# Time-mix and mixture-of-experts kernel: how the last batch's expert rows come back to their tokens

## The chip, the cores and the metric

The kernel runs on one core of one Trainium2 chip. A core has five engines with instruction streams of their own: TensorE (PE, matmuls into the banks of PSUM), VectorE (DVE), ScalarE (ACT), GpSimd (POOL) and SyncE (SP, which here only issues DMAs). They meet through semaphores. Sixteen DMA engines move data between the on-chip memory and DRAM; SP and POOL both hand them work. The metric is the device time of one launch in microseconds, median of three runs.

## The reference, cut to what matters

```python
x = layernorm(x + time_mix(x))            # (4, 1024, 128), two layers, a scan over time in each
# per batch of 1024 tokens: 8 experts, the best K = 2 for each token, cap = int(1.2*2*1024/8) = 307 slots
top2, ei = top_k(x @ router_w + router_b, 2);  probs = softmax(top2)
pos = running count of each expert's picks, all first choices before all second ones
expert_inputs = zeros(8, cap, 128).at[ei, pos].add(x)
o = (silu((xe @ w_fc + b_fc) * (xe @ w_gate + b_gate)) @ w_proj) + b_proj
y[token] = sum over k of probs[k] * o[ei[k], pos[k]]      # an index past cap reads row cap - 1
out = layernorm(x + y)
```

## The kernel before

Four batches go through the kernel one behind another. After a head (time mixing of batches 0 and 1, weights split into a high and a low part), the program is four **passes**, one for each batch. A pass has 32 **points**: point 4e + j computes columns 128j to 128j + 127 of the hidden layer of expert e, as six matmuls into a pair of PSUM banks (`hidden_pair`), a copy with bias on ACT (`gate_copy`), and a product on DVE (`product`, L1053), which frees the banks for the point after next. Four tables (`TENSOR_...`, `SCALAR_...`, `VECTOR_...` and POOL's own) say what else each engine does at which point: time mixing of the batch after next, routing of the next batch, and the combining of batches already computed. So the order is written out by hand on each engine, and a wait on one instruction holds all that stand behind it.

The way of a batch b through DRAM has four legs:

- **Scatter** (POOL, `scatter`, L1160): 16 indirect DMAs write the tokens' normalized rows `x_ln` into `slot_rows` by expert slot, one for 128 tokens and one of their two choices. They stand at points 9 to 24 of pass b - 1. SP then loads `slot_rows` in five groups (`load_slots`, L386), PE turns three of these at points 28 to 30, and two in the next pass.
- **Store** (SP, `store_expert`, L394): each expert's 312 slots by 128 outputs are copied from PSUM by DVE (`copy_out`, L1062, as 104 partitions by 3 rows, in a ring of three buffers `o_sb`) and stored plainly into `expert_rows`. The copy of expert e stands at point 4(e + 2); those of experts 6 and 7 stand at points 0 and 2 of the next pass, or behind the last pass.
- **Gather** (POOL, `gather`, L1182): 16 indirect DMAs bring back, for 128 tokens and one choice each, the rows that these tokens need, from `expert_rows` into `picked`. The first waits until all eight experts are stored. A gather into quarter q of `picked` also waits until the earlier output of that quarter has been stored.
- **Combine** (`gather_sum`, L1018 to L1034, and `final_norm`, L1041, on DVE; `final_rstd`, L1193 and L1197, on POOL; `store_out`, L398, on SP): share times row plus `x_ln`, mean and variance, normalization, output, by quarters of two tiles of 128 tokens.

Batches 0 to 2 gather and combine inside later passes. For batch 3 nothing is left to hide behind: its 16 gathers stand after pass 3 on POOL, then its combining, then four output stores.

POOL is kept in step with the points by `pace(b, point)`, which waits for the product of the point before. `FILL` lists spare matmuls that PE runs at a few places where it would stand idle.

## Time and profile before

| | us |
|---|---|
| median of three runs | 389.23 (389.17 to 389.45) |
| the profiled execution: its own time | 389.6 |
| the profiled execution: span from first to last instruction | 387.9 |
| busy in the span: PE, DVE, POOL, ACT | 323.1, 261.8, 186.8, 168.3 |
| chain that ended last: PE 55%, DVE 14%, issue 11%, POOL 8%, DMA 6%, ACT 4% of the span | |
| the 64 gathers (L1182) on POOL: busy, mean of one | 66.2, 1.035 |
| the 64 scatters (L1160) on POOL: busy, mean of one | 72.0, 1.125 |

The span leaves out what lies around the first and the last instruction, 1.7 us here. PE is busy for 83% of the span, but that is an average: in the last tenth it hardly works. The share by engine of the chain says how the span was spent when each moment is put down to what the end depended on. Busy time of POOL for an indirect DMA is only the time in which POOL prepares it; the data move afterwards.

### The profile page before, as it was taken

The numbers are of one execution on the slowest core, as the hardware profiler recorded it, in microseconds if no ns is written. First come the engines' busy times: TensorE is split into PE (matmuls) and PEld (weight loads), VectorE is DVE, ScalarE is ACT, GpSimd is POOL, SyncE is SP. The second block draws the span as 40 slices with busy tenths as digits, with TensorE's granted clock in tenths as the row PEclk, the third lists the DMA queues.
The fourth block names the chain that finished last, engine by engine and source line by source line (L and its number), as shares of the span: only waits on it lengthen the run. The fifth ranks groups of instructions, "written<-read, shape, count | busy, mean of one in ns | idle before, by whom it ended". The sixth has DMA issues, their size and how long they took to land.

```text
span 387.9 us, 6844 instructions
## 1 busy us (share of the span) xinstructions
PE 323.1 (83%) x2193; PEld 269.7 (70%) x2193; DVE 261.8 (68%) x846; ACT 168.3 (43%) x309; POOL 186.8 (48%) x225
## 2 busy tenths in 40 slices
PE   6978877679899999999999999989999897795000
PEld 3434544346888969999798899989989797794000
DVE  6496774767966877979788778894546775751234
ACT  2535424444554544545446453545454544451000
POOL 5021315772234473324646557747746667200674
PEclk9999969999999999999999999999999999999555
DMA  7615963414013113211111161123262132121112
GB/s 221 186 55 58 199 184 93 130 36 140 3 32 97 37 47 112 71 41 46 49 44 48 44 184 54 49 64 100 76 178 78 41 96 76 48 60 33 41 50 71
DMA packets 53058, 31.73 MB, mean 82 GB/s; under 512 B 12704, under 2 KB 48807, under 8 KB 53024
## 3 DMA queue, kind: packets, MB, share of 16 engines
q1 hardware_dynamic: 47840, 22.99, 21.8%
q0 software_dynamic: 4096, 8.06, 7.2%
q10 hardware_dynamic: 1088, 0.26, 0.4%
q8 instruction: 17, 0.28, 0.3%
q14 instruction: 17, 0.14, 0.1%
HBM read 18.92 MB, written 12.71 MB: 82 GB/s over the span
## 4 chain that ended last, share of the span: by engine, by line
PE 55%; DVE 14%; issue 11%; POOL 8%; DMA 6%; ACT 4%; SPq 0%; DVEq 0%; POOLq 0%; ACTq 0%
PE ps_o L647 14%; POOL slot_rows L1160 4%; POOL picked L1182 3%; PE bank L499 3%; PE bank L507 3%; DMA picked<-expert_rows,row_from 2%; PE bank L509 2%; PE pair0g L633 2%; DVE prod L1053 2%; DVE kv_sb L899 2%; DMA slot_rows<-x_ln,row_to 2%; PE pair1h L578 2%; PE bank L611 2%; PE pair1g L633 2%; DMA slot_x<-slot_rows 2%
## 5 line engine op out<-in xcount | busy, mean ns | idle before, releaser
L647 PE MATMUL ps_o<-proj_sb,hidden 128*104 128x128 f32 x744 | 94.0, 274 | 2.1 <-DVE o_sb L1062 2.1
L1160 POOL DMA_INDIRECT slot_rows<-x_ln,row_to x64 | 72.0, 1125 | 42.9 <-DVE prod L1053 24.4
L1182 POOL DMA_INDIRECT picked<-expert_rows,row_from x64 | 66.2, 1035 | 53.4 <-DVE prod L1053 18.7
L647 PEld LDWEIGHTS ps_o<-proj_sb,hidden 128*104 128x104 f32 x744 | 87.3, 170 | 4.1 <-issue 2.5
L772 ACT ACTIVATE gate_s<-pair0g,bgate_sb 128x308 f32<-128x308 f32 x64 | 33.1, 516 | 81.5 <-PE pair0g L635 81.5
L1053 DVE SCALAR_TENSOR_TENSOR prod<-pair1h,bfc_sb,gate_s 128x308 f32<-128x308 f32 x64 | 34.0, 531 | 23.3 <-ACT gate_s L772 22.8
L779 ACT ACTIVATE hidden<-prod 128x616 f32<-128x616 f32 x64 | 45.5, 710 | 9.3 <-DVE prod L1053 9.3
L1053 DVE SCALAR_TENSOR_TENSOR prod<-pair0h,bfc_sb,gate_s 128x308 f32<-128x308 f32 x64 | 34.0, 531 | 19.7 <-ACT gate_s L772 18.9
L772 ACT ACTIVATE gate_s<-pair1g,bgate_sb 128x308 f32<-128x308 f32 x64 | 32.9, 514 | 20.1 <-PE pair1g L635 19.6
L1135 POOL TENSOR_SCALAR shifted<-moments 128x4 f32<-128x4 f32 x24 | 5.6, 231 | 69.2 <-DVE moments L856 69.1
L633 PE MATMUL pair1g<-slotT_hi,gate_hi 128*128 128x308 f32 x64 | 26.1, 408 | 4.9 <-DVE prod L1053 4.9
L633 PE MATMUL pair0g<-slotT_hi,gate_hi 128*128 128x308 f32 x64 | 25.6, 400 | 0.9 <-DVE prod L1053 0.5
L1139 POOL TENSOR_TENSOR rstd<-shifted,power 128x4 f32<-128x4 f32 x24 | 25.0, 1041 | 2.0
L1018 DVE SCALAR_TENSOR_TENSOR picked<-picked,share,x_ln 128x128 f32<-128x128 f32 x30 | 9.2, 346 | 20.3 <-DMA picked<-expert_rows,row_from 20.3
L1062 DVE TENSOR_TENSOR o_sb<-ps_o,bproj_sb 104x384 f32<-104x384 f32 x32 | 17.5, 547 | 6.6 <-PE ps_o L647 3.2
L930 DVE TENSOR_TENSOR slotT_lo<-bank,slotT_hi 128x512 fp32r<-128x512 f32 x20 | 13.8, 689 | 11.9 <-ACT slotT_hi L756 11.7
L578 PE MATMUL pair1h<-x_ln,ident 128*128 128x512 f32 x32 | 17.0, 613 | 5.8 <-ACT fc_hi L763 4.2
L899 DVE TENSOR_TENSOR_SCAN kv_sb<-decay,kv_sb 128x512 f32<-128x512 f32 x16 | 20.0, 1253 | 0.4
L635 PE MATMUL pair1g<-slotT_hi,gate_lo 128*128 128x308 f32 x64 | 19.5, 305 | 0.0
L633 PE MATMUL pair0h<-slotT_hi,fc_hi 128*128 128x308 f32 x64 | 19.5, 305 | 0.0
L634 PE MATMUL pair1h<-slotT_lo,fc_hi 128*128 128x308 f32 x64 | 19.5, 305 | 0.0
L633 PE MATMUL pair1h<-slotT_hi,fc_hi 128*128 128x308 f32 x64 | 19.5, 305 | 0.0
(155 smaller groups left out, 725.5 us busy)
## 6 DMA issues: line engine op xcount, KB each, us to landing
slot_x<-slot_rows SPq DMA_DIRECT2D x20, 256.0 KB, 3.3
expert_rows<-o_sb SPq DMA_DIRECT2D x32, 156.0 KB
x_in<-in_L_attn_h SPq DMA_DIRECT2D x4, 512.0 KB, 4.8
x_ln<-in_L_ffn_w_gate SPq DMA_DIRECT2D x8, 256.0 KB, 3.7
x_ln<-in_L_ffn_w_c_fc SPq DMA_DIRECT2D x8, 256.0 KB, 4.1
proj_sb<-in_L_ffn_w_c_proj SPq DMA_DIRECT2D x8, 256.0 KB, 5.4
out<-picked SPq DMA_DIRECT2D x16, 128.0 KB, 2.1
slot_rows<-slot_x SPq DMA_DIRECT2D x5, 256.0 KB, 4.4
```

The costliest lines, as they stand in the source:

```text
L578: nc.tensor.matmul(pair[1][1][:, :], ident[:, :], w_in[:, e % 2, H * which:H * which + H], start=True, stop=False)
L633: nc.tensor.matmul(ps, hi[:, e, chunk], slotT_hi[:, cols], start=True, stop=False)
L634: nc.tensor.matmul(ps, hi[:, e, chunk], slotT_lo[:, cols], start=False, stop=False)
L635: nc.tensor.matmul(ps, lo[:, e, chunk], slotT_hi[:, cols], start=False, stop=True).then_inc(made, 1)
L647: mm = nc.tensor.matmul(ps_o[0:PART, P * part:P * part + P], hidden[:, e % 2, c, PART * part:PART * part + PART], proj_sb[:, e, c, :], sta ...
L772: nc.scalar.activation(gate_s[:, c % 2, :], pair[c % 2][0][:, 0:COLS], ACT.Identity, bias=bgate_sb[:, e, j:j + 1]).then_inc(g_copied, 1)
L779: nc.scalar.activation(hidden[:, e % 2, 2 * i:2 * i + 2, 0:COLS], prod[:, e % 2, 2 * i:2 * i + 2, :], ACT.Silu).then_inc(hidden_made, 1)
L899: nc.vector.tensor_tensor_scan(kv_sb[:, lo:hi], decay[:, :], kv_sb[:, lo:hi], kv_sb[:, lo - 1:lo] if n % 2 else 0.0, ALU.mult, ALU.add)\
L1053: nc.vector.scalar_tensor_tensor(prod[:, e % 2, j, :], pair[c % 2][1][:, 0:COLS], bfc_sb[:, e, j:j + 1], gate_s[:, c % 2, :], ALU.add, ALU ...
L1139: nc.gpsimd.tensor_tensor(rstd[:, r, norm, tiles], shifted[:, r, norm, tiles], power[:, 0:HT], ALU.pow)\
L1160: nc.gpsimd.indirect_dma_start(out=slot_rows, out_offset=bass.IndirectOffsetOnAxis(ap=row_to[:, c:c + 1], axis=0), in_=x_ln[:, b % RING, c ...
L1182: nc.gpsimd.indirect_dma_start(out=picked[:, j, k, :], out_offset=None, in_=expert_rows[b % 2], in_offset=bass.IndirectOffsetOnAxis(ap=row ...
```

## The change

The last batch (`LAST`, pass 3) takes another way back. Its expert outputs are not stored by slot and gathered by token, but **sent** by slot to the place of their token, and then loaded plainly.

1. Each row of `x_ln`, of the slot buffer and of `slot_rows` becomes 129 numbers long. The additional one (`homes`) is the token's place in a new DRAM tensor `returned` (2048 rows of 128, two for each token), or a far value for batches 0 to 2 and for empty slots. So the scatter carries each slot's home along. The expert weights that are loaded into the same memory in the head now land in pieces of 128 numbers.
2. SP loads these numbers (`load_homes`, 104 by 24 numbers of 4 bytes each from rows 516 bytes apart) at the end of pass 2. DVE adds 1 where the slot's number is not below the count of first choices of its expert (`homes_of`); PE gets this count by 8 more matmuls in `count`.
3. DVE clears a buffer at point 14 of pass 2 (`blank`) and SP writes it twice over `returned` (1 MB in all, `blank_returned`), after the store of expert 4 and ahead of the slot loads of batch 3.
4. In pass 3 POOL sends each expert's three times 104 rows (`send_back`) at points 4(e + 2) to 4(e + 2) + 2, those of experts 6 and 7 behind the pass. SP stores no `expert_rows` there, but moves one row of each expert, the one that tokens past the capacity read (`load_last_row`).
5. Tokens past the capacity get their share of that row by a matmul: `over_of` on DVE, `turn_over` and `add_over` on PE, `copy_over` on ACT.
6. Behind the pass SP loads `returned` in four plain DMAs of 256 KB (`load_picks`). PE adds up in PSUM: `keep` puts in `x_ln` (identity times tile), `add_picks` adds two products for each tile with diagonal matrices of the shares (`scales_of`, 128 by 1024 each, on DVE at points 12 and 16). DVE takes statistics and norm from PSUM (`last_stats`, `last_norm`). Twenty spare matmuls stand before `add_picks`.
7. The combining of batch 2 moves: its gathers stand at points 4 to 7 and 9, 11, ... 31 of pass 3, its sums of quarters 0 to 2 at points 10, 18 and 26 (they were at 10, 14, 18 and 22), and the fourth behind the pass. The gathers of batch 1 move from pass 3 into pass 2 (points 21 to 31). In pass 2 the scatters are allowed at points 9 to 20 in place of 9 to 24.
8. `picks`, `y_out`, `scale` and others lie in memory that is free by then (`x_mid`, `x_in`, `mixed`, `kv_sb`), and `x_ln` has a buffer for each batch, as before (four).

```diff
-RING = 4
+RING = B
...
-GATHERS_LAST = {**{p: (2, 12 + p) for p in range(0, 4)}, **{p: (1, p - 4) for p in range(4, 20)}}
+GATHERS_LAST = {**{p: (1, p - 4) for p in range(4, 8)}, **{9 + 2 * i: (1, 4 + i) for i in range(12)}}
+GATHERS_AHEAD = {**{p: (2, 12 + p) for p in range(0, 4)}, **{p: (1, p - 4) for p in range(4, 9)},
+                 **{p: (1, p - 16) for p in range(21, 32)}}
 POOL_COMBINE = {10: [(1, 0)], 29: [(1, 1)], 3: [(2, 2)], 7: [(2, 3)]}
-POOL_COMBINE_LAST = {3: [(2, 2)], 7: [(2, 3)], 10: [(1, 0)], 14: [(1, 1)], 18: [(1, 2)], 22: [(1, 3)]}
+POOL_COMBINE_LAST = {1: [(2, 2)], 5: [(2, 3)], 11: [(1, 0)], 19: [(1, 1)], 27: [(1, 2)]}
...
+RETURNS = {4 * (e + 2) + i: (e, i) for e in range(6) for i in range(PARTS)}
+TENSOR_LAST = {9: [("keep", 0)], 11: [("keep", 1)], 20: [("turn_over", 0)], 22: [("turn_over", 1)], 24: [("keep", 2)]}
+SCALAR_LAST = {21: [("copy_over", 0)], 23: [("copy_over", 1)]}
+VECTOR_LAST = {1: [("over", 0)], 5: [("homes", 0)], 12: [("scales", 0)], 16: [("scales", 1)]}
...
-        x_ln = sb("x_ln", [P, RING, TILES, P])
+        x_rows = sb("x_rows", [P, RING, TILES, P + 1])
+        x_ln = x_rows[:, :, :, 0:P]
+        homes = x_rows[:, :, :, P:P + 1]
...
-        slot_x = sb("slot_x", [P, SLOT_RING, 4, P])
+        slot_in = sb("slot_in", [P, SLOT_RING, 4, P + 1])
+        slot_x = slot_in[:, :, :, 0:P]
...
+        picks = x_mid[:, :, :, :].rearrange("p r (o j) d -> p (r o) j d", j=K)
+        y_out = x_in[:, 1, :, :]
+        overs = row_in[:, 0:TILES * E]
+        oversT = normT[0:E, :]
+        last_rows = normed[0:E, 0, :]
+        scale = [held[:, :].rearrange("p (j d) -> p j d", d=P) for held in (mixed, kv_sb)]
...
-                sp.dma_start(w_in[:, e % 2, 0:H], w_gate[e]).then_inc(expert_weights_in[e % 2], 16)
-                sp.dma_start(w_in[:, e % 2, H:2 * H], w_fc[e]).then_inc(expert_weights_in[e % 2], 16)
+                sp.dma_start(w_in[:, e % 2, 0:HC, :], w_gate[e].rearrange("p (j d) -> p j d", d=P)).then_inc(expert_weights_in[e % 2], 16)
...
+            def load_homes():
+                sp.wait_ge(scattered, nth(LAST, 16 * TILES * K, 16 * TILES * K))
+                with nc.allow_non_contiguous_dma("one number of each row"):
+                    sp.dma_start(home_f[:, :], home_view).then_inc(home_in, 16)
+            def blank_returned():
+                sp.wait_ge(blank_made, 1)
+                for i in range(2):
+                    sp.dma_start(blank_view[i], x_in[:, 0, :, :].rearrange("p j d -> p (j d)"))\
+                      .then_inc(returned_blank, 16)
+            def load_last_row(e):
+                sp.wait_ge(o_copied, nth(LAST, E, e + 1))
+                i = (LAST * E + e) % OUT_RING
+                sp.dma_start(last_rows[e:e + 1, :], o_sb[LAST_ROW:LAST_ROW + 1, i, LAST_PART, :])\
+                  .then_inc(last_row_in[i], 16)
+            def load_picks(q):
+                for i in range(OUT_RING):
+                    sp.wait_ge(sent_back[i], 16 * PARTS * last_experts(i))
+                sp.dma_start(picks[:, QT * q:QT * q + QT, :, :].rearrange("p j k d -> p j (k d)"),
+                             returned_view[:, QT * q:QT * q + QT, :]).then_inc(picks_in[q], 16)
...
+                    for j in range(TILES):
+                        mm = nc.tensor.matmul(route_banks(b)[1][:, TILES * K * E:TILES * K * E + E], ones[:, :],
+                                              chosen[:, j, 0, :], start=False, stop=(j == TILES - 1),
+                                              skip_group_check=True)
...
+            def keep(q):
+                if q < 3:
+                    pe.wait_ge(slots_copied, nth(LAST, GROUPS, (3, 4, 5)[q]))
+                if q == 2:
+                    pe.wait_ge(over_copied, 2)
+                if q == 3:
+                    pe.wait_ge(g_copied, nth(LAST, POINTS, POINTS - 1))
+                for i in range(QT):
+                    nc.tensor.matmul(sums(q)[:, P * i:P * i + P], ident[:, :], x_ln[:, LAST, QT * q + i, :],
+                                     start=(i == 0), stop=False, skip_group_check=True)
+            def turn_over(half):
+                pe.wait_ge(over_step, 3)
+                if half == 0:
+                    pe.wait_ge(slots_copied, nth(LAST, GROUPS, 5))
+                else:
+                    pe.wait_ge(over_copied, 1)
+                for i in range(HT):
+                    j = HT * half + i
+                    mm = nc.tensor.transpose(bank[1][0:E, P * i:P * i + P], overs[:, E * j:E * j + E], ident[:, :])
+                mm.then_inc(over_turned, 1)
+            def add_over(q):
+                if q == 0:
+                    for i in range(OUT_RING):
+                        pe.wait_ge(last_row_in[i], 16 * last_experts(i))
+                for i in range(QT):
+                    j = QT * q + i
+                    nc.tensor.matmul(sums(q)[:, P * i:P * i + P], oversT[:, P * j:P * j + P], last_rows,
+                                     start=False, stop=False, skip_group_check=True)
+            def add_picks(q):
+                pe.wait_ge(scale_made, 2)
+                pe.wait_ge(picks_in[q], 16)
+                for i in range(QT):
+                    j = QT * q + i
+                    for k in range(K):
+                        mm = nc.tensor.matmul(sums(q)[:, P * i:P * i + P], scale[k][:, j, :], picks[:, j, k, :],
+                                              start=False, stop=(k == K - 1), skip_group_check=True)
+                mm.then_inc(summed, 1)
...
+            keep(QUARTERS - 1)
+            for q in range(QUARTERS):
+                add_over(q)
+            pe.wait_ge(g_copied, nth(LAST, POINTS, POINTS))
+            fill("picks", LAST, 0, pair[1][0])
+            for q in range(QUARTERS):
+                add_picks(q)
...
+            def blank():
+                dve.wait_ge(normed_made[1], step(LAST - 1, 5))
+                nc.vector.memset(x_in[:, 0, :, :], 0.0).then_inc(blank_made, 1)
...
+                nc.vector.tensor_tensor(second[:, :].rearrange("p (e i) -> p e i", i=PARTS),
+                                        place[:, :].rearrange("p (e i) -> p e i", i=PARTS),
+                                        firsts[0:PART, :].rearrange("p (e o) -> p e o", o=1).to_broadcast([PART, E, PARTS]),
+                                        ALU.is_ge).then_inc(home_step, 1)
+                dve.wait_ge(home_step, 1)
+                dve.wait_ge(home_in, 16)
+                nc.vector.tensor_tensor(second[:, :], second[:, :], home_f[:, :], ALU.add).then_inc(home_step, 1)
+                dve.wait_ge(home_step, 2)
+                nc.vector.tensor_copy(home[:, :], second[:, :]).then_inc(home_made, 1)
...
+            def scales_of(k):
+                nc.vector.tensor_tensor(scale[k], ident[:, :].rearrange("p (o d) -> p o d", o=1).to_broadcast([P, TILES, P]),
+                                        share[:, LAST, :, k:k + 1].to_broadcast([P, TILES, P]), ALU.mult)\
+                  .then_inc(scale_made, 1)
...
+            def last_stats(q):
+                dve.wait_ge(summed, q + 1)
+                for i in range(QT):
+                    mm = nc.vector.bn_stats(y_stats[:, QT * q + i, :], sums(q)[:, P * i:P * i + P])
+                mm.then_inc(y_stats_made, 1)
+                dve.wait_ge(y_stats_made, nth(LAST, QUARTERS, q + 1))
+                for j in range(QT * q, QT * q + QT):
+                    mm = nc.vector.bn_aggr(y_moments[:, j, :], y_stats[:, j, :])
+                mm.then_inc(y_moments_made, 1)
...
-                    in_=x_ln[:, b % RING, c // K, :], in_offset=None, bounds_check=ROWS - 1, oob_is_err=False)\
+                    in_=x_rows[:, b, c // K, :], in_offset=None, bounds_check=ROWS - 1, oob_is_err=False)\
                   .then_inc(scattered, 16)
+            def send_back(e, i):
+                c = LAST * E + e
+                if e == 0 and i == 0:
+                    pool.wait_ge(home_made, 1)
+                    pool.wait_ge(returned_blank, 16 * 2)
+                if i == 0:
+                    pool.wait_ge(o_copied, nth(LAST, E, e + 1))
+                nc.gpsimd.indirect_dma_start(
+                    out=returned,
+                    out_offset=bass.IndirectOffsetOnAxis(ap=home[:, PARTS * e + i:PARTS * e + i + 1], axis=0),
+                    in_=o_sb[:, c % OUT_RING, i, :], in_offset=None, bounds_check=K * T - 1, oob_is_err=False)\
+                  .then_inc(sent_back[c % OUT_RING], 16)
...
+            nc.gpsimd.memset(slot_in[:, 0, :, P:P + 1], FAR).then_inc(zeroed, 1)
...
+            nc.gpsimd.memset(homes[:, 0:LAST, :, :], FAR).then_inc(homes_made, 1)
+            nc.gpsimd.iota(homes[:, LAST, :, :].rearrange("p j o -> p (j o)"), pattern=[[K * P, TILES]], base=0,
+                           channel_multiplier=K, allow_small_or_imprecise_dtypes=True).then_inc(homes_made, 1)
+            nc.gpsimd.iota(place[:, :], pattern=[[0, E], [PART, PARTS]], base=0, channel_multiplier=1,
+                           allow_small_or_imprecise_dtypes=True).then_inc(homes_made, 1)
...
-            for c in range(K * TILES):
-                gather(B - 1, c)
+            for e in range(E - 2, E):
+                for i in range(PARTS):
+                    send_back(e, i)
+            final_rstd(LAST - 1, QUARTERS - 1)
```

The order of POOL in pass 3, before, points 4 to 14. The names: `picked<-expert_rows` is a gather, `returned<-o_sb` a send, `y_shifted` and `y_rstd` are the two instructions of one `final_rstd`.

```order
L1182 DMA picked<-expert_rows,row_from 128x128 x4
L1193 TENSOR_SCALAR y_shifted<-y_moments 128x2
L1197 TENSOR_TENSOR y_rstd<-y_shifted,power 128x2
L1182 DMA picked<-expert_rows,row_from 128x128 x3
L1193 TENSOR_SCALAR y_shifted<-y_moments 128x2
L1197 TENSOR_TENSOR y_rstd<-y_shifted,power 128x2
L1182 DMA picked<-expert_rows,row_from 128x128 x4
```

And after, the same engine, points 4 to 13 of pass 3.

```order
L1423 DMA picked<-expert_rows,row_from 128x128 x2
L1433 TENSOR_SCALAR y_shifted<-y_moments 128x2
L1437 TENSOR_TENSOR y_rstd<-y_shifted,power 128x2
L1423 DMA picked<-expert_rows,row_from 128x128 x2
L1400 DMA returned<-o_sb,home 2048x128
L1423 DMA picked<-expert_rows,row_from 128x128
L1400 DMA returned<-o_sb,home 2048x128 x2
L1423 DMA picked<-expert_rows,row_from 128x128
L1433 TENSOR_SCALAR y_shifted<-y_moments 128x2
L1437 TENSOR_TENSOR y_rstd<-y_shifted,power 128x2
L1400 DMA returned<-o_sb,home 2048x128
L1423 DMA picked<-expert_rows,row_from 128x128
```

Where one gather stood at each point up to point 19, there are now, from point 8 to the end of the pass, two gathers and three sends for every four points.

The end of POOL's program, before.

```order
L1182 DMA picked<-expert_rows,row_from 128x128 x16
L1193 TENSOR_SCALAR y_shifted<-y_moments 128x6
L1197 TENSOR_TENSOR y_rstd<-y_shifted,power 128x6
L1193 TENSOR_SCALAR y_shifted<-y_moments 128x2
L1197 TENSOR_TENSOR y_rstd<-y_shifted,power 128x2
```

And after; the row of six sends is experts 6 and 7.

```order
L1400 DMA returned<-o_sb,home 2048x128 x2
L1423 DMA picked<-expert_rows,row_from 128x128
L1400 DMA returned<-o_sb,home 2048x128 x6
L1433 TENSOR_SCALAR y_shifted<-y_moments 128x2
L1437 TENSOR_TENSOR y_rstd<-y_shifted,power 128x2
L1433 TENSOR_SCALAR y_shifted<-y_moments 128x6
L1437 TENSOR_TENSOR y_rstd<-y_shifted,power 128x6
L1433 TENSOR_SCALAR y_shifted<-y_moments 128x2
L1437 TENSOR_TENSOR y_rstd<-y_shifted,power 128x2
```

Sixteen gathers behind the pass became six sends, and one `final_rstd` of batch 2 came in behind them.

SP around the boundary of passes 2 and 3, before: `expert_rows<-o_sb` is an expert's store, `slot_x<-slot_rows` a slot load.

```order
L394 DMA expert_rows<-o_sb 104x3x128 x2
L386 DMA slot_x<-slot_rows 128x4x128 x3
L394 DMA expert_rows<-o_sb 104x3x128
L386 DMA slot_x<-slot_rows 128x4x128 x2
L394 DMA expert_rows<-o_sb 104x3x128 x3
```

And after.

```order
L480 DMA expert_rows<-o_sb 104x3x128 x2
L459 DMA returned<-x_in 128x1024 x2
L449 DMA slot_in<-slot_rows 128x4x129 x3
L480 DMA expert_rows<-o_sb 104x3x128
L449 DMA slot_in<-slot_rows 128x4x129 x2
L454 DMA home_f<-slot_rows 104x24x1
L480 DMA expert_rows<-o_sb 104x3x128 x2
```

The two writes of 512 KB came in ahead of the slot loads, and the load of the homes behind them.

## Rows read from the trace of the kernel before

**Rows 1.** Two windows at the end: busy us and instructions by engine, clock, DMA, GB/s.
```profile
300.00:340.00 40.00, 33.93 (x258) 32.37 (x258) 27.99 (x87) 18.39 (x35) 23.57 (x30) 1.00 0.25 67
...
352.00:388.00 36.00, 2.62 (x24) 2.41 (x23) 10.88 (x41) 0.00 (x0) 18.84 (x20) 0.58 0.19 53
```

**Rows 2.** Timeline, last 37 us: start, us, engine, line, operation [idle before, releaser].
```profile
351.14 0.56 DVE L1062 TENSOR_TENSOR o_sb<-ps_o,bproj_sb 104x384 f32<-104x384 f32 x1
...
351.75 2.87 PE L661 MATMUL ps_o<-proj_sb,hidden 128*104 128x128 f32 x24 [0.65 <-DVE o_sb L1062]
354.65 0.56 DVE L1062 TENSOR_TENSOR o_sb<-ps_o,bproj_sb 104x384 f32<-104x384 f32 x1 [2.96 <-PE ps_o L661]
358.10 1.11 POOL L1182 DMA_INDIRECT picked<-expert_rows,row_from  x1 [18.02 <-DMA expert_rows<-o_sb]
...
367.19 0.49 DVE L1030 BATCH_NORM_STATS2 y_stats<-picked 128x6 f32<-128x128 f32 x2
...
367.71 0.25 DVE L1034 BATCH_NORM_AGGREGATE y_moments<-y_stats 128x2 f32<-128x6 f32 x2
...
379.04 1.00 POOL L1182 DMA_INDIRECT picked<-expert_rows,row_from  x1 [0.30 <-issue]
...
380.48 1.36 POOL L1197 TENSOR_TENSOR y_rstd<-y_shifted,power 128x6 f32<-128x6 f32 x1
381.55 0.35 DVE L1072 SCALAR_TENSOR_TENSOR picked<-picked,share,x_ln 128x128 f32<-128x128 f32 x1 [1.22 <-DMA picked<-expert_rows,row_from]
...
382.75 2.13 DVE L1041 TENSOR_SCALAR picked<-picked,y_moments,y_rstd 128x128 f32<-128x128 f32 x8
...
383.25 0.79 POOL L1197 TENSOR_TENSOR y_rstd<-y_shifted,power 128x2 f32<-128x2 f32 x1
383.36 1.98 SPq L398 DMA_DIRECT2D out<-picked  x4
```

**Rows 3.** Chain that ended last, two stretches: start us, us, what.
```profile
85.27 2.77 DMA slot_rows<-x_ln,row_to
...
279.68 3.81 DMA slot_rows<-x_ln,row_to
...
283.51 2.83 DMA slot_x<-slot_rows
```

**Rows 4.** Timeline of POOL, passes 2 and 3.
```profile
259.31 1.03 POOL L1160 DMA_INDIRECT slot_rows<-x_ln,row_to  x1 [0.31 <-issue]
...
279.68 0.97 POOL L1160 DMA_INDIRECT slot_rows<-x_ln,row_to  x1 [0.30 <-issue]
...
313.68 1.11 POOL L1182 DMA_INDIRECT picked<-expert_rows,row_from  x1 [2.70 <-DVE prod L1053]
...
317.45 0.23 POOL L1193 TENSOR_SCALAR y_shifted<-y_moments 128x2 f32<-128x2 f32 x1
317.77 0.72 POOL L1197 TENSOR_TENSOR y_rstd<-y_shifted,power 128x2 f32<-128x2 f32 x1
318.69 1.17 POOL L1182 DMA_INDIRECT picked<-expert_rows,row_from  x1 [0.20 <-issue]
```

**Rows 5.** Timeline of DVE, pass 3: a sum waits for its gather.
```profile
321.53 0.61 DVE L1018 SCALAR_TENSOR_TENSOR picked<-picked,share,x_ln 128x128 f32<-128x128 f32 x2 [1.95 <-DMA picked<-expert_rows,row_from]
```

**Rows 6.** Timeline of SP, the second store of batch 1.
```profile
310.73 0.93 SPq L398 DMA_DIRECT2D out<-picked  x2
```

**Rows 7.** Page, DMA queues and issues: packets, MB, share; KB, us to landing.
```profile
q1 hardware_dynamic: 47840, 22.99, 21.8%
...
bfc_sb<-in_L_ffn_b_c_fc SPq DMA_DIRECT2D x1, 16.0 KB, 5.0
```

**Rows 8.** Lines of DVE: names, shapes, count, busy us, mean ns, idle.
```profile
L880 DVE TENSOR_TENSOR x_in<-x_in,x_mid 128x1024 f32<-128x1024 f32 x4 | 4.9, 1217 | 0.0
```

**Rows 9.** Windows of 2 us: granted clock is the third number from the right.
```profile
356.00:358.00 2.00, 0.00 (x0) 0.00 (x0) 0.00 (x0) 0.00 (x0) 0.00 (x0) 1.00 0.29 80
358.00:360.00 2.00, 0.00 (x0) 0.00 (x0) 0.00 (x0) 0.00 (x0) 1.11 (x1) 0.50 0.05 16
```

More of the change, by code:

```diff
@@ L669, in period @@
                     hidden_pair(b, e, j)
+                    if b == LAST:
+                        for name, n in TENSOR_LAST.get(point, ()):
+                            last_stages[name](n)
                     if b + 1 < B:
@@ L1096, in period @@
                             slots_low(b + ahead, g)
+                    if b + 1 == LAST and point == 14:
+                        blank()
+                    if b == LAST:
+                        for name, n in VECTOR_LAST.get(point, ()):
+                            last_stages[name](n)
                     for name, behind, q in (VECTOR_COMBINE if b + 1 < B else VECTOR_COMBINE_LAST).get(point, ()):
```

172 lines of the change are left out of this document (125 added, 47 removed).

## The prediction

> **What bounds the kernel now.** I read the windows first. From 300 to 340 us PE is busy for 33.9 of 40 us; from 352 us on for 2.6 of 36, while POOL is busy for 18.8 and DVE for 10.9 [rows 1]. So the last tenth of the span has another limit than the rest, and the change aims at it. The timeline says which: DVE copies the last expert's outputs at 354.65, POOL starts its first gather at 358.10 and its sixteenth at 379.04, and all of DVE's work there waits for gathers [rows 2]. A gather costs POOL 1.00 us and 0.30 before the next. Behind the sixteenth come its landing (DVE starts at 381.55), sum and statistics, `final_rstd`, the norms (to 384.88) and the output store, 3.0 us to the span's end at 387.9 [rows 2]. From the end of the last copy (355.21) to the end of the span it is 32.7 us, about 21 of it POOL's issuing of gathers.
>
> The chain shows what else the end hangs on. POOL issues scatters without a gap worth naming from 259.31 to 279.68; the last one has landed after 3.81 us, the first slot load takes 2.83, and only then PE can turn slots for pass 3 [rows 3, 4]. Whatever delays scatter or load there delays everything behind.
>
> **The change part by part: the tail.** Removed are the last store with its wait (355.21 to 358.10) and 16 gathers. In their place is a queue of sends on POOL, most of it beside PE's work in pass 3. When does that queue end?
>
> Before, the first gather of batch 2's second quarter starts at 313.68 though it stands at point 8; POOL had waited 2.7 us [rows 4]. I put the wait down to the output stores issued at 310.73 [rows 6], for which this gather must wait and which the changed kernel has at the same place. From there POOL has 12 gathers, 3 `final_rstd` and 17 sends in the pass, and 6 sends behind it. A gather is 1.31 us with its gap. A `final_rstd` took 317.45 to 318.69, with the gap, 1.24 [rows 4], say 1.27. A send of 104 rows is not in the trace. Its upper bound is a scatter of 128 rows, 0.97 + 0.31 = 1.28 [rows 4]; its lower bound is 104/128 of the 0.97, and the gap, 1.10. I take 1.20, the middle, a little up since the first DMA behind another kind of work takes 0.1 more (1.11 and 1.17 against 1.00) [rows 2, 4]. Sum: 12 x 1.31 + 3 x 1.27 + 17 x 1.20 + 6 x 1.20 = 15.7 + 3.8 + 20.4 + 7.2 = 47.1 us. With the start at 313.7 the queue ends at 360.8; the bounds of the send make it 358.5 to 362.6. The other condition is the last copy: it ends at 355.2, and three sends behind it end at 358.8. So POOL's queue decides, by 2 us. Whatever PE or DVE lose in pass 3 up to 2 us is then hidden.
>
> The Trainium skill (DMA: Bandwidth & Descriptors, section "Anatomy of one DMA") puts the cost of generating descriptors down as small, with a fixed part that does not grow with size. By that a send costs what a scatter of 128 rows costs, and the sum ends 23 x 0.08 = 1.8 us later than with my value. No row here has another number of rows than 128.
>
> Behind the queue:
> - The last send starts 1.2 before the end of the queue and has landed 2.8 later (2.77 for a scatter in the head; 3.81 beside gathers is the upper bound) [rows 3]: 362.4.
> - Four loads of 256 KB. The nearest row is a slot load of the same size, 2.83 to its landing [rows 3]. The data of one are 512 packets, at 28.3 ns each on one of 16 engines (21.8% of 16 x 387.9 us over 47,840 packets [rows 7]) 0.9 us; `returned` has pieces twice as long, so 0.8. The fourth is there at 362.4 + 2.8 + 3 x 0.8 = 367.6, the third at 366.8.
> - Each quarter needs four matmuls of 128 x 128 (2.87/24 = 0.12 each, with fill-in and fill-out 0.6) and 0.49 + 0.25 + gaps of statistics, 0.8 [rows 2]. Third quarter's moments 368.2, fourth's 369.0.
> - `final_rstd` of three quarters: 0.23 + 1.36 and gaps, 1.9 [rows 2, 4], to 370.1; of the fourth 0.23 + 0.79 and gaps, 1.1, to 371.2. Then two norms, 0.7: 371.9.
> - 3.0 to the span's end as before: 374.9.
>
> The other work of the tail lies beside the sends and loads: the combining of batch 2's fourth quarter (2 us of DVE at 356, one `final_rstd` behind the sends, before 362.4), `keep`, `add_over` and the 20 spare matmuls on PE. The last row's move lands at about 358 (a store issued behind the last copy, at 355.2, lets POOL go at 358.10 [rows 2]), then 8 matmuls and 20 spare ones, 5 to 6 us at full clock, 364, before the first picks (365.2).
>
> TensorE's granted clock was 1.00 up to 358 and 0.50 behind it, with PE idle since 354.62 [rows 2, 9]. PE now works again at about 358, so the fall may come or not; if `add_picks` runs at 1.2 GHz in place of 2.4, it costs 0.5.
>
> **The rest of the program.**
> - Head: POOL has one more small clearing before the constants that PE's first matmul waits for, 0.2. The weights land in pieces of 512 bytes in place of 2048; the loads are waited for once, so 0 to 0.5. I take 0.3 for both.
> - Boundary of passes 2 and 3: 8 small matmuls and a copy in the routing, on the way to the scatters, 0.3. The scatters are allowed earlier, but POOL already runs them back to back [rows 4], so nothing comes of that. The 1 MB of blank rows is issued at about 279.2, in the very microsecond of the last scatters. At 28.3 ns for 512 bytes it would take 3.6 us of all engines, so it is through at about 284; the last scatters share the engines with it, and the first slot load is issued at 283.5. Bounds 0 and 3.6; I take 0.8, because most of the time is covered by the scatter's own 3.81. The rows of 516 bytes make load and scatter longer by 1% by size; 0 to 0.5, I take 0.2.
> - The homes are 2496 numbers of 4 bytes; 4096 such numbers of the biases took 5.0 us to land [rows 7]. Issued at about 290 they are there at 296, and DVE wants them at point 5, after 303. Nothing, covered by 7 us.
> - Pass 3, DVE: the two `scales_of` are as long as the 1.22 us of a 128 x 1024 addition [rows 8], the small ones 1.5 together; one combining of 2 us leaves the pass, and before it two waits for gathers (1.95 is one) [rows 5]. PE gets about 22 small matmuls, 2 us. But the sum at point 18 now needs the fourth gather from 313.7, behind 3 gathers, 5 sends and a `final_rstd`: start 313.7 + 3.9 + 6.0 + 1.3 = 324.9, landed at 327.5, where DVE would ask for it at about 324. So DVE waits 3 us there. This is the new wait; the pass as a whole ends about where it ended, since DVE's sums of before took as much. I take +0.5 for the last copy, hidden behind POOL's queue.
>
> What moves POOL's start at 313.7 moves the end: 0.3 + 0.3 + 0.8 + 0.2 = 1.6, less 0.4 for the sums at points 1 and 5, which now stand where DVE idles anyway: **+1.2**. Span 374.9 + 1.2 = 376.1; with the 1.7 us around it 377.8, to be held against 389.6 of the profiled execution, which is 0.4 above the median of the runs (389.23). So **377.4 us**, 11.8 less than before.
>
> The Trainium skill (same page, section "How a descriptor splits into AXI transactions") speaks against rows of 516 bytes: a transaction starts at a 256-byte boundary, so a row that starts elsewhere costs additional ones (its example of 576 bytes goes from 18 beats to 25). By that the 0.9 us of data of a slot load would become up to 1.4, and the boundary 0.5 later than by size, the end with it. No row here has rows that start off such a boundary.
>
> **The rivals.**
> 1. POOL's queue in pass 3 is too full. A send costs 1.28 or more (gather and send in turn, each 0.1 dearer), DVE's waits at points 18 and 26 grow, and the last copy slips by more than 2 us. For it: POOL has 5 DMAs, 6.2 us, in four points; from the sum of point 14 (321.53) to the copy behind point 31 (351.14) [rows 2, 5] a point takes 1.7, four of them 6.9, and every second four have a `final_rstd` of 1.3 too. Against: the queue may lag to the end of the pass at no cost. Sends at 1.28 alone give 379.2, the rest up to 381.5.
> 2. The transfers at the boundary. Blank rows ahead of slot loads, 4-byte pieces ahead of the store of expert 6, each on the same queue: the full 3.6 and another 1 or 2. Against: there the engines are mostly idle. 381 to 383.
> 3. The tail is cheaper: sends at 1.10 and the start not moved. Then the last copy decides: 374 to 375.
> 4. Slower. Rows of 129 numbers are cut in two, so that a scatter costs POOL twice the preparation. Place: POOL's run of 16 scatters to 279.68, which is on the chain, and the last five in the head. Price 0.97 x 21 = 20 us: 397. It decides from 0.6 us more for each scatter (12/21). For it: no row has such a length. Against: the work is by row, and their number stays.
> 5. The change does not take the gathers off the end: with the order above that cannot be; six sends stand there.
>
> **How the numbers follow.** Forecast 0.58 (376 to 379), rival 1 0.20, rival 2 0.10, rival 3 0.07, rival 4 with all that loses over 12 us 0.04, something that eats the gain just so 0.01. The range of eight in ten leaves out rival 4 and the ends of 2 and 3: 374.2 to 382. Under 0.2% (0.8 us) a measurement can't tell a change from none. Faster 0.95, same 0.01, slower 0.04.
>
> **What would show it.** The last POOL DMA starts at 360 to 363, not at 379; the sends' mean is 0.8 to 1.0 us; the first `picks` matmul starts at about 366; behind the last norm 3 us. DVE waits at point 18 for `picked`. PE's first slot turn of pass 3 starts at 287 to 288. The forecast is wrong if a scatter's mean leaves 0.97, if the slot turn comes after 289.5, or if PE's busy share of pass 3 falls under that of rows 1.

## The result, and the profile after

The changed kernel took **385.55 us** (median of four runs, 382.97 to 385.58) beside 389.34 for the kernel before (389.17 to 391.3): ratio 0.9862, 95% interval 0.9833 to 0.9891, so 1.4% faster. I had forecast 377.4 with a range of 374.2 to 382.0: the direction was right, the size was not. Two thirds of the 11.8 us did not come. The profiled execution took 385.53, its span is 383.7.

The page first: busy time, then POOL's three kinds of indirect DMA (line, engine, operation, count, busy us, mean ns, idle before).

```profile
PE 340.7 (89%) x2293; PEld 283.0 (74%) x2293; DVE 261.5 (68%) x840; ACT 169.3 (44%) x311; POOL 196.1 (51%) x237
...
L1388 POOL DMA_INDIRECT slot_rows<-x_rows,row_to x64 | 71.5, 1117 | 43.5 <-DVE prod L1224 22.8
...
L1423 POOL DMA_INDIRECT picked<-expert_rows,row_from x48 | 50.3, 1047 | 29.3 <-DVE prod L1224 16.8
...
L1400 POOL DMA_INDIRECT returned<-o_sb,home x24 | 25.4, 1058 | 7.1 <-issue 6.2
```

A scatter costs POOL what it cost (1.125 before), and a send of 104 rows as much as a gather of 128, 1.058. The last POOL DMA now starts at 365.72 and not at 379.04 [rows 2]; I had said 360 to 363. The chain shows two places that are late, and the first is far from the tail. Chain that ended last, start and duration:

```profile
280.69 6.16 DMA slot_rows<-x_rows,row_to
286.86 3.16 DMA slot_in<-slot_rows
...
365.72 2.12 DMA returned<-o_sb,home
...
368.88 4.50 DMA x_mid<-returned
```

The last scatter of batch 3 took 3.81 us to land before [rows 3], and takes 6.16 now. What SP issued meanwhile, and what PE met, in the timeline:

```profile
280.69 0.90 SPq L459 DMA_DIRECT2D returned<-x_in  x2
286.86 1.48 SPq L449 DMA_DIRECT2D slot_in<-slot_rows  x3
...
290.15 1.07 PE L711 MATMUL bank<-ident,slot_in 128*128 128x128 f32 x4 [3.38 <-DMA slot_in<-slot_rows]
```

The 1 MB of blank rows (L459) is issued in the same instant as the last scatter, and the DMA engines are full behind it (the last two numbers are their mean busy share and GB/s):

```profile
282.00:284.00 2.00, 2.00 (x20) 2.00 (x18) 0.78 (x2) 1.07 (x2) 1.70 (x2) 1.00 1.06 412
```

In the kernel before, the same window has a share of 0.13 and 35 GB/s. At 412 GB/s 1 MB takes 2.5 us, an estimate from this row, and the landing is 2.35 longer. PE waits 3.38 us for slots (0.87 before) and turns them at 290.15, beyond the 289.5 that I had named as the mark of a wrong forecast. Right behind the wait its clock is down (windows of 2 us; the clock is the third number from the right), and later once more, in the middle of `add_picks`:

```profile
290.00:292.00 2.00, 1.84 (x8) 1.88 (x9) 0.10 (x1) 0.60 (x1) 1.70 (x2) 0.54 0.89 251
292.00:294.00 2.00, 2.00 (x12) 2.00 (x12) 1.13 (x2) 0.52 (x1) 1.18 (x2) 0.60 0.81 225
...
372.00:374.00 2.00, 1.69 (x9) 1.42 (x8) 1.34 (x8) 0.00 (x0) 0.00 (x0) 0.52 0.71 233
```

The first `product` of pass 3 comes 5.3 us later than before; at the end of pass 2 the two kernels were 1.2 apart. So the boundary, from the end of pass 2 to the first product of pass 3, costs 4.1 us. Pass 3 makes some of it up: from 300 to 340 us PE is busy for 38.76 of 40 us where it was 33.93 [rows 1], and the last `copy_out` starts at 357.62, 3.0 later than before. But POOL can't make it up. It waits for the product of its point and is behind from there (timeline of POOL; the gather at 316.14 answers to the one at 313.68 in [rows 4]):

```profile
307.54 1.11 POOL L1423 DMA_INDIRECT picked<-expert_rows,row_from  x1 [2.45 <-DVE prod L1224]
...
316.14 1.03 POOL L1423 DMA_INDIRECT picked<-expert_rows,row_from  x1 [0.61 <-issue]
...
365.72 0.99 POOL L1400 DMA_INDIRECT returned<-o_sb,home  x1 [0.31 <-issue]
```

Then the tail, in place of [rows 2]:

```profile
367.89 1.91 SPq L471 DMA_DIRECT2D x_mid<-returned  x4
...
370.71 0.46 PE L807 MATMUL bank<-x_mid,mixed 128*128 128x128 f32 x2 [2.68 <-DMA x_mid<-returned]
...
373.52 0.77 PE L807 MATMUL bank<-x_mid,mixed 128*128 128x128 f32 x2 [0.31 <-DMA x_mid<-returned]
...
376.86 1.35 POOL L1437 TENSOR_TENSOR y_rstd<-y_shifted,power 128x6 f32<-128x6 f32 x1
...
378.25 2.00 DVE L1300 TENSOR_SCALAR x_in<-bank,y_moments,y_rstd 128x128 f32<-128x128 f32 x6 [0.94 <-POOL y_rstd L1437]
...
380.17 0.72 DVE L1300 TENSOR_SCALAR x_in<-pair0g,y_moments,y_rstd 128x128 f32<-128x128 f32 x2
```

From the issue of the loads to the end of the span it is 15.8 us; I had 12.5. So the gap between forecast and trace has two halves: the loads are issued 4.3 late (367.89 against 363.6), and what follows them takes 3.3 more.

### The profile page after: what moved, and what is told of

It reads as the page before. It is cut to its first block, busy times and chain, and to the rows that moved or that the text cites. A ratio compares the mean times of both kernels' runs of the same rounds, so it can differ in the third digit from the quotient of the medians.

```text
span 383.7 us, 7087 instructions
## 1 busy us (share of the span) xinstructions
PE 340.7 (89%) x2293; PEld 283.0 (74%) x2293; DVE 261.5 (68%) x840; ACT 169.3 (44%) x311; POOL 196.1 (51%) x237
## 4 chain that ended last, share of the span: by engine, by line
PE 60%; DVE 12%; issue 9%; DMA 8%; POOL 7%; ACT 4%; SPq 0%; DVEq 0%; POOLq 0%; ACTq 0%
PE ps_o L747 16%; PE bank L594 3%; PE bank L602 3%; DMA slot_rows<-x_rows,row_to 2%; PE pair0g L733 2%; PE bank L604 2%; POOL slot_rows L1388 2%; POOL returned L1400 2%; PE pair1g L733 2%; DVE kv_sb L1067 2%; DVE prod L1224 2%; PE pair0g L735 2%; DMA slot_in<-slot_rows 2%; PE pair0g L734 2%; PE bank L711 2%
## 5 line engine op out<-in xcount | busy, mean ns | idle before, releaser
L1388 POOL DMA_INDIRECT slot_rows<-x_rows,row_to x64 | 71.5, 1117 | 43.5 <-DVE prod L1224 22.8
L1423 POOL DMA_INDIRECT picked<-expert_rows,row_from x48 | 50.3, 1047 | 29.3 <-DVE prod L1224 16.8
L1400 POOL DMA_INDIRECT returned<-o_sb,home x24 | 25.4, 1058 | 7.1 <-issue 6.2
L1098 DVE TENSOR_TENSOR slotT_lo<-bank,slotT_hi 128x512 fp32r<-128x512 f32 x20 | 13.8, 689 | 15.1 <-ACT slotT_hi L913 14.9
L678 PE MATMUL pair1h<-x_rows,ident 128*128 128x512 f32 x32 | 17.0, 613 | 5.8 <-ACT fc_hi L920 4.2
L735 PE MATMUL pair1h<-slotT_hi,fc_lo 128*128 128x308 f32 x64 | 19.6, 306 | 0.0
```

Source lines behind the costliest of these rows:

```text
L735: nc.tensor.matmul(ps, lo[:, e, chunk], slotT_hi[:, cols], start=False, stop=True).then_inc(made, 1)
L1388: nc.gpsimd.indirect_dma_start(out=slot_rows, out_offset=bass.IndirectOffsetOnAxis(ap=row_to[:, c:c + 1], axis=0), in_=x_rows[:, b, c // K ...
L1400: nc.gpsimd.indirect_dma_start(out=returned, out_offset=bass.IndirectOffsetOnAxis(ap=home[:, PARTS * e + i:PARTS * e + i + 1], axis=0), in ...
L1423: nc.gpsimd.indirect_dma_start(out=picked[:, j, k, :], out_offset=None, in_=expert_rows[b % 2], in_offset=bass.IndirectOffsetOnAxis(ap=row ...
```

## The experiments

Theory A: the blank rows hold up the last scatters, the boundary slips by 4, and POOL's queue hands that on to the end; its queue is 3 to 4 us longer than I reckoned. The rivals were rows of 516 bytes as the cost (B), another limit behind POOL's queue (C), a delay that needs these rows or the fuller queue beside the writes (D), and, later, on a send's price: it does not depend on its rows (E), or it falls with them (F).

**early_blank**: the same writes half a pass earlier.

```diff
-                    if e == 4 and b + 2 == B:
+                    if e == 1 and b + 2 == B:
                         blank_returned()
...
-                    if b + 1 == LAST and point == 14:
+                    if b + 1 == LAST and point == 2:
                         blank()
```

> The changed kernel, with the clearing at point 2 and the two 512 KB writes over the place rows at expert 1 (point 12) of pass 2 in place of expert 4 (point 24). Theory A: these writes, issued in the microsecond of the last scatters, share the 16 DMA engines with them and stand in front of the slot loads, and so made the boundary 4 us longer. Then the last scatter lands 3.8 us after its start again (6.2 with the change), PE waits about 1 us for the first slots in place of 3.4, the granted clock does not fall there, and the last send on POOL starts 2 to 4 us earlier: 381.5 to 383.5 us. Theory B: the boundary is longer through the rows of 516 bytes or the 4-byte loads of the homes. Then landing and wait stay as they are: 385 to 386 us.

Measured: 380.09 us (380.01 to 380.2), ratio 0.9739 [0.9716, 0.9761] to the kernel before. Its chain at the boundary:

```profile
280.87 3.67 DMA slot_rows<-x_rows,row_to
284.56 2.62 DMA slot_in<-slot_rows
...
287.32 0.63 PE bank L711 x4
```

The landing is back at 3.7, PE waits 0.59, and its clock stays up there. The window from 282 to 284 has a DMA share of 0.35 and 91 GB/s. The first product of pass 3 is 0.85 behind the kernel before in place of 5.3, the last send starts at 361.35 in place of 365.72 (4.4 earlier), the loads are issued at 363.53, and the end is 14.9 behind that in place of 15.8, since `add_picks` ran at full clock. So A holds, and moving two lines of SP and DVE work gave 5.3 us of span, more than I had expected (380.09 lies under my 381.5 to 383.5): I had left out what the lowered clock costs. The boundary shows what the queue does with a delay: here pass 3 starts 4.4 earlier and POOL ends 4.4 earlier.

**before_with_blank**: the kernel before with these writes and nothing else of the change.

```diff
+            def blank_returned():
+                sp.wait_ge(blank_made, 1)
+                for i in range(2):
+                    sp.dma_start(blank_view[i], x_in[:, 0, :, :].rearrange("p j d -> p (j d)"))\
+                      .then_inc(returned_blank, 16)
...
+                    if e == 4 and b + 2 == B:
+                        blank_returned()
```

> The kernel before, with nothing of the change but the 1 MB of blank rows (cleared at point 14 of pass 2, written behind the store of expert 4; nobody reads them). Theory A (these writes alone hold up the last scatters): the last scatter lands about 6.2 us after its start in place of 3.8, the first slot turn of pass 3 starts 2 to 3.5 us later than in the kernel before (286.5), TensorE's clock falls at the boundary as in the changed kernel, and the end is 3.5 to 5 us later: 393 to 395. Theory D (the delay needs the 516-byte rows or POOL's fuller queue as well): landing and turn stay within 1 us, 389 to 390.5.

Measured: 395.71 us (395.03 to 396.97) against 390.34, ratio 1.013 [1.009, 1.017]. Chain and timeline at the boundary:

```profile
283.18 6.22 DMA slot_rows<-x_ln,row_to
289.42 3.11 DMA slot_x<-slot_rows
...
292.66 1.04 PE bank L623 x4
```

In the profiled execution TensorE's clock fell at 101.6 us as well, before any blank row, which put everything behind it 3.5 late (0.54 in the window 101 to 108); that part is not the edit's. From the end of pass 2 to the first product of pass 3 it lost another 4.3 us, with PE waiting 3.56 and its clock at 0.68 and 0.50 in the windows behind. So the writes do it alone; wide rows and a fuller queue aren't needed. Of the 4.3, 2.4 is the landing (6.22 against 3.81), 0.3 the load (3.11 against 2.83), and the rest falls in the stretch at the low clock. D fell. The ratio gives 5.1 us in all, a little over the 3.5 to 5 expected; how much of it the writes cost in the three executions that were not profiled (395.03 to 396.19) is open. The full DMA engines of the window above fit writes and scatter sharing the engines; no run tells this from contention in the DRAM.

**wide_rows**: the kernel before with rows of 129 numbers, and weights in pieces of 128.

```diff
-        x_ln = sb("x_ln", [P, RING, TILES, P])
+        x_rows = sb("x_rows", [P, RING, TILES, P + 1])
+        x_ln = x_rows[:, :, :, 0:P]
...
-        slot_rows = nc.dram_tensor("slot_rows", [ROWS, P], F32, kind="Internal").ap()
+        slot_rows = nc.dram_tensor("slot_rows", [ROWS, P + 1], F32, kind="Internal").ap()
```

> The kernel before, with the rows of 129 numbers alone (x_ln, slot buffer, slot_rows, the weights landing in 512-byte pieces), nothing of the new way back. Theory A: it costs the 0.8 us seen at the start of pass 0 and 0.1 to 0.3 at each boundary: 390.1 to 391 us. Theory B (the rows make scatters and slot loads slow): about 4 us more at the last boundary: 393 to 394 us.

Measured: 391.81 us (390.38 to 394.51) against 389.95, ratio 1.0041 [1.0022, 1.006]: 1.6 us by the ratio, 1.9 by the medians, between the two expectations. The boundary shows none of it: last scatter to landing 3.69, load 2.91 (3.81 and 2.83 before), slot turn at 285.95. B fell. What the profiled execution lost came behind point 16 of pass 3, in a stretch at the low clock. Just ahead of it PE had waited for DVE, which had waited 1.86 for a gather (the wait of [rows 5]):

```profile
323.75 0.41 PE L636 MATMUL pair1g<-slotT_hi,gate_hi 128*128 128x308 f32 x1 [2.25 <-DVE prod L1056]
```

```profile
322.00:324.00 2.00, 0.25 (x2) 0.26 (x3) 1.93 (x8) 0.27 (x1) 1.59 (x4) 1.00 0.18 33
...
324.00:326.00 2.00, 2.00 (x15) 2.00 (x14) 1.50 (x5) 0.97 (x2) 1.72 (x2) 0.78 0.54 135
326.00:328.00 2.00, 2.00 (x10) 2.00 (x10) 0.36 (x2) 0.99 (x2) 1.48 (x2) 0.50 0.42 86
```

The kernel before waits 2.00 us at the same matmul, and there the clock stayed at 1.00. So rows of 516 bytes cost about nothing where I looked for them. They may cost that a wait of 2.0 becomes one of 2.25 and the clock falls behind it, but no run shows that the rows are the reason. Whether that is the whole 1.6 stays open too: one execution was profiled, and the kernel before itself ranged from 389.2 to 392.5 in these comparisons.

**late_gathers**: the last four gathers of batch 2 go behind the last send, and this quarter is combined between the statistics and the norms of batch 3. That takes four instructions, 5.4 us, out of POOL's queue ahead of the last send. (With own semaphores and small buffers, left out here.)

```diff
-GATHERS_LAST = {..., **{9 + 2 * i: (1, 4 + i) for i in range(12)}}
+GATHERS_LAST = {..., **{9 + 2 * i: (1, 4 + i) for i in range(8)}}
...
-            final_rstd(LAST - 1, QUARTERS - 1)
+            for c in range(K * QT * (QUARTERS - 1), K * TILES):
+                gather(LAST - 1, c)
```

> The changed kernel, with the last four gathers of batch 2 (points 25, 27, 29, 31) behind the last send, and the combining of that quarter between the statistics and the norms of batch 3. Theory A: POOL's queue sets the end, so the last send starts up to 5.4 us earlier (4 x 1.34), but not before the last copy and two sends, so near 361.5 in place of 365.7; the quarter's sum on DVE gives 1 us back: 381 to 383 us. Theory C: what counts is fixed behind the last copy (loads, statistics, norms), and the queue is not on the path: 385 us or more, since DVE has 3 us more to do at the end.

Measured: 381.43 us (380.46 to 382.22), ratio 0.9771 [0.9746, 0.9796]. The last send starts at 361.90, 3.8 earlier, with the boundary as slow as in the changed kernel (landing 6.07). So POOL's queue had set the time of the last send: C fell. Of the 5.4 us taken out 3.8 came at the last send, because the queue is now short enough to meet another limit. POOL waits for the copy of expert 6, and behind it stand six sends without a gap (timeline of POOL):

```profile
355.41 0.99 POOL L1446 DMA_INDIRECT returned<-o_sb,home  x1 [1.88 <-DVE o_sb L1247]
...
361.90 0.99 POOL L1446 DMA_INDIRECT returned<-o_sb,home  x1 [0.30 <-issue]
```

The late gathers and the second combining cost 0.5 of it back (16.3 from loads to end in place of 15.8).

**early_and_late**: both edits together, those of early_blank and of late_gathers.

> Both of the above. If boundary and queue are two costs (theory A), pass 3 is earlier by up to 4 us and POOL's queue no longer decides: the last copy does, and two sends behind it: 378 to 380.5 us. If the two are one cost (the queue only hides what the boundary gives), it is as late_gathers alone: 381 to 383 us.

Measured: **377.86 us** (377.3 to 378.27), ratio 0.9685 [0.9663, 0.9708]: 3.15% faster than the kernel before, just under the 378 to 380.5 of theory A, and the best of this study. The two gains add up for the most part: the span is 383.7 with neither edit, 378.4 and 380.4 with one, 375.5 with both (8.2 of 5.3 + 3.3; by the medians 7.7 of 5.5 + 4.1). Two different causes, then, in one queue:

```profile
357.15 0.99 POOL L1446 DMA_INDIRECT returned<-o_sb,home  x1 [0.31 <-issue]
...
359.34 1.91 SPq L479 DMA_DIRECT2D x_mid<-returned  x4
...
370.55 2.29 SPq L496 DMA_DIRECT2D out<-x_in  x4
```

POOL's wait for the copy of expert 6 is there too (1.89 at 350.64), and from this send to the last one it is five steps of 1.30. So the limit has moved: from POOL's queue through the whole pass to PE's and DVE's time for expert 6 and the six sends behind it. By this row a fifth instruction moved out of the queue would bring nothing; it wasn't run.

**short_sends**: sends of 64 rows in place of 104. Rows 64 to 103 of each third are not sent back, so this part of the result is left out.

```diff
-                    out_offset=bass.IndirectOffsetOnAxis(ap=home[:, PARTS * e + i:PARTS * e + i + 1], axis=0),
-                    in_=o_sb[:, c % OUT_RING, i, :], in_offset=None, ...
+                    out_offset=bass.IndirectOffsetOnAxis(ap=home[0:64, PARTS * e + i:PARTS * e + i + 1], axis=0),
+                    in_=o_sb[0:64, c % OUT_RING, i, :], in_offset=None, ...
```

> The changed kernel with sends of 64 rows in place of 104: rows 64 to 103 of each third are not sent back (that part of the result is left out). Theory E (what POOL spends on an indirect DMA does not depend on the rows): the sends' mean stays at 1.00 to 1.06, the last send starts at 365 to 366, the time stays within 0.5 of 385.5. Theory F (it grows with the rows, as my lower bound of 104/128 supposed): the mean falls to about 0.65, 23 sends are 9 us shorter, and the last copy decides when the last send starts (about 361): 380 to 381.5.

Measured: 379.86 us, a single execution. Its sends on the profile's page, and the last ones in the timeline:

```profile
L1400 POOL DMA_INDIRECT returned<-o_sb,home x24 | 22.5, 936 | 7.0 <-issue 6.1 <-DVE o_sb L1236 0.6 <-DVE prod L1224 0.3
...
358.88 0.90 POOL L1400 DMA_INDIRECT returned<-o_sb,home  x1 [0.31 <-issue]
...
361.30 0.90 POOL L1400 DMA_INDIRECT returned<-o_sb,home  x1 [0.30 <-issue]
```

A send behind a send takes 0.90 in place of 0.99: 40 rows fewer save 0.09 to 0.10 us, 2.4 ns a row, and if the two sizes are taken as a line, an estimate, some 0.75 us are left that don't depend on rows. (The line does not reach the scatters and gathers, which take 0.97 and 1.00 for 128 rows.) The mean of 0.936 is under E's 1.00 to 1.06, but far from F's 0.65: a small part grows with the rows. Yet the time fell as F had it. The trace gives the parts: the span is 5.6 shorter, of which 1.6 is an earlier start of the gather that I reckon from (314.55 in place of 316.14; the landing at the boundary took 5.45 this time, though nothing there was edited), 2.8 POOL's queue from there to the last send (46.75 in place of 49.58), 0.1 the landing, and 1.1 behind the loads, with `add_picks` at full clock. So my expectation for E was wrong in its time: 24 sends at 0.12 less are 2.9 us, and I had put 0.5. Some 0.9 of these 2.9 are one send, the sixth, which takes 1.83 to 1.85 in each profiled execution with 104 rows and 0.91 here; why is not shown (single scatters take up to 1.93 too).

**after_again**: the changed kernel, without any edit.

> The changed kernel unchanged, on the chip of these experiments: 385.3 to 385.8 if its time is as steady as the three of its four runs that agree; executions near 383 if the one at 382.97 is a second outcome, in which TensorE's clock is not lowered at the boundary of passes 2 and 3 (then its mean clock is 0.98 and not 0.97).

Measured: 384.57 us (382.74 to 385.11), ratio 0.9836 [0.9802, 0.987]. Of its ten executions in both comparisons seven lie at 384.3 to 385.6 and three at 382.7 to 383.1. In the profiled one the landing took 6.12 and the clock fell at the boundary as before; the loads were issued later still (368.61), but it ended 0.5 earlier, since `add_picks` ran at full clock. So the time is not as steady as I had put it (385.3 to 385.8). Of the three at 383 none was profiled; their mean granted clocks are 0.979, 0.975 and 0.973, those of the other seven 0.970 to 0.973. That does not tell which fall of the clock was missing, if one was: short_sends has 0.979 with the fall at the boundary.

**no_spare**: early_and_late without the 20 spare matmuls.

```diff
-..., ("slots", 0, 0): 10, ("picks", LAST, 0): 20}
+..., ("slots", 0, 0): 10}
```

> early_and_late without its 20 spare matmuls ahead of the picks. If they keep the clock up for add_picks: those 32 matmuls run at a granted clock of 0.50, four of a tile's take about twice as long (0.8 to 1.6 for two tiles), and the end is 1 to 2.5 us later than early_and_late (377.9): 379 to 380.5. If the loads set the pace and the matmuls have slack between them: within 0.5 of 377.9.

Measured: 380.07 us (378.72 to 380.44), ratio 0.9738 [0.97, 0.9776] in place of 0.9685. PE now idles before the picks, and they run at the low clock:

```profile
362.84 0.76 PE L818 MATMUL bank<-x_mid,mixed 128*128 128x128 f32 x2 [5.18 <-DMA x_mid<-returned]
363.40 0.63 PE L818 MATMUL bank<-x_mid,kv_sb 128*128 128x128 f32 x2
...
367.05 0.39 PE L818 MATMUL bank<-x_mid,mixed 128*128 128x128 f32 x2
```

0.63 for a pair of matmuls in place of 0.39. The spare matmuls earn 1.4 (spans of the profiled executions) to 2.2 us (medians of two comparisons, beside a kernel before at 389.95 and 390.34) there, more than the 0.5 that I had given the clock. They hold nothing up: with them the first picks start at 362.78, without them at 362.84.

## Why the prediction was wrong

By its own steps:

- **What bounds the kernel, and what goes**: right. The 16 gathers and the last store's wait left the tail, six sends stand there, POOL's queue and not the last copy decides. Rival 4 (129 numbers cut in two) fell: the scatters' mean is 1.117 beside 1.125. Rival 3 (a cheaper tail) fell as well.
- **The boundary, "bounds 0 and 3.6; I take 0.8"**: the failed step. I argued that the scatter's own 3.81 covers the writes. It doesn't: the landing grew with what was issued beside it, to 5.45 to 6.22 in all five executions with the writes there, and was 3.60 to 4.01 in the five without. It measured 2.4 more in the landing and 0.3 in the load, and then the part that was missing from the sum altogether: PE, idle for 3.4 us, came back with its clock at 0.54, which makes it 4.1 (4.3 in before_with_blank). At the last send it is 4.4 us (early_blank), where the sum has 0.8. The bound of 3.6 was near the answer. Rival 2 had this mechanism, at 381 to 383, and I gave it 0.10.
- **The start of POOL's queue, "+1.2"**: 316.14 in place of 314.9, only +1.2 more although the pass began 4.1 late. That the error is small is luck: it is made of two larger ones of opposite sign. I had put the start at 313.7 down to the output stores and taken it over. But in early_blank, without the writes at the boundary, the same gather starts at 311.75, 2.4 before the 314.1 that the sum gives without its 0.8 for them. The writes then add 4.4 and not 0.8. In the changed kernel the queue itself sets this start, behind the product that POOL waited for at 307.54, and it has no wait of a microsecond from there on; before, it had stood there for 2.7 us [rows 4].
- **The queue, 47.1 us for 12 gathers, 3 `final_rstd` and 23 sends**: 50.9, a second step that failed. A send costs 1.058 + 0.30 = 1.36, not 1.20: 23 x 0.16 = 3.7 us. My middle between "as the rows" and "as a scatter" was too low, and so was its upper bound of 1.28: 104 rows cost a send 0.99 to 1.01 behind another send, and 1.02 to 1.09 behind a gather or a `final_rstd`; one took 1.83 (at 326.86), which is 0.8 of the 3.7. Rival 1 had "sends at 1.28 or more", at 0.20. The Trainium skill (DMA: Bandwidth & Descriptors, section "Anatomy of one DMA") counts the generating of descriptors to the cost of a DMA that does not grow with size. I had reckoned 1.8 us by it and not taken it. short_sends agrees for the most part: by the estimate above 0.75 of 0.99 us does not grow with the rows.
- **The landing of the last send, "2.8"**: 2.17, 0.6 better.
- **Behind the loads, "12.5"**: 15.8, the third step. At full clock (short_sends) it is 14.7, and there the terms can be laid side by side, counted from the issue of the loads, forecast first. The third quarter's data: 4.4 and 5.4. Its moments: 5.8 and 7.4; a quarter's sums and statistics take more than the 1.4 that I had from data to moments. `final_rstd` of three quarters: 7.7 and 9.2. Then the norms, nearly as large a piece as the data: I let those of three quarters run beside and counted two at the end; but the six wait for the rstd of all three quarters and take 2.00, and the other two 0.72, so the norms end at 11.9 where I had 9.5. Behind them 2.9 (3.0). The last 1.1 of the changed kernel is `add_picks` at the clock of 0.52 and 0.62; I had priced that at 0.5 if it came.
- **Pass 3**: DVE's wait for `picked` at point 18 was 0.25 and not the 3 us forecast, and 1.35 at point 26. The late boundary is not the reason, for in early_blank they are 0.26 and 1.33: there the gather starts at 324.60, as forecast (324.9), but DVE asks for it at 326.96 and not at about 324. The last copy came 3.0 late and not 0.5, hidden behind the queue as I had said.
- **Homes, head**: the homes were hidden. The head is 0.8 late in place of 0.3, but in the other profiled executions it ends from 0.7 earlier (wide_rows) to 0.9 later (early_blank) than before, so it can't be told apart. The 0.5 us that the prediction named for rows off a boundary did not show: the first slot load without the writes took 2.62 to 2.92 in four executions with rows of 516 bytes, and 2.83 before.

In the sum: 1.2 (start, made of 3.6 for the boundary and -2.4 for the start of before), 3.7 (queue), -0.6 (landing), 3.3 (behind the loads) make 7.6 us, which is 383.7 less the 376.1 of the forecast.

early_and_late says what the change is worth when boundary and queue are mended: 377.86, close to the figure that I had given the change as it stood. That is luck and no merit of the forecast, as the tail behind the loads is still longer than in its sum.

## What to carry to other kernels

A bulk write that nobody waits for is not free if a landing on the chain falls in the same microseconds: look in the timeline for what is issued beside the chain's DMAs, and move the write to where the chain holds compute. Where an in-order queue runs without waits, count its instructions and price each as a whole one of the nearest kind (40 of 104 rows fewer took a tenth off here), then ask what of it must stand ahead of the last one that matters. When a queue is shortened, look for the wait that turns up in it: from there on, further shortening is lost. And a wait of 2 to 4 us on TensorE can cost more than itself, for the clock comes back later than the data (1.4 to 1.6 us at this boundary): put it in the sum, at the boundary as in the tail.

## What the runs showed of the hardware

- An indirect DMA behind another of its kind costs POOL about 1 us almost whatever its rows: 64 rows 0.90 and 104 rows 0.99 (send), 128 rows mostly 0.99 to 1.02 (gather) and 0.97 to 0.98 (scatter), and 0.30 between two. Single ones took up to 1.93.
- 1 MB of plain writes issued beside the last indirect scatter lengthened its landing to 6.07 to 6.22 us in four profiled executions (5.45 in a fifth); in five without them it was 3.60 to 4.01.
- TensorE's clock fell to its lower level (1.2 of 2.4 GHz, 0.50) at the boundary in the five executions with a wait of 2.31 (short_sends) to 3.56 us there, and not in the five with one of 0.59 to 1.07. In pass 3 it fell behind one of 2.25 and not behind one of 2.00 at the same matmul. In the tail it fell behind one of 2.68 (the changed kernel) and not behind one of 2.79 (early_blank), so the length of the wait alone does not decide. It fell once at 101 us too (before_with_blank), where the longest wait shortly before was 1.17.
- Rows of 516 bytes in place of 512 cost the first slot load nothing that can be seen: 2.62 to 2.92 us in four executions without the writes beside it, against 2.83. Nor did they cost POOL anything in a scatter (mean 1.117 against 1.125).
